# Two maximum tiles of a pair of steps as 64-row matmuls on the two halves of TensorE's rows, in a fused attention and feed-forward kernel

## The reference

```
q, k, v = (einsum('bsd,dhk->bshk', LN(x), W) + b  for q, k, v)
scores  = einsum('bqhk,bshk->bhqs', q, k) / sqrt(64)
attn    = softmax(scores)                       # over 2048 keys
ctx     = einsum('bhqs,bshk->bqhk', attn, v)
y       = LN(x) + einsum('bqhk,hkd->bqd', ctx, Wo) + bo
x       = x + LN(LN(y) * gamma + beta)
h       = silu(LN(x) @ wg.T) * (LN(x) @ wu.T)   # hidden width 768
out     = x + LN(h @ wd.T)
```

## Time and profile before

| | us |
|---|---|
| median of 3 runs | 2895.32 (2895.0 to 2895.43) |
| profiled execution, its own time | 2896.84 |
| its span | 2895.0 |
| opening, to about | 91 |
| 32 heads, about | 91 to 2472 |
| feed-forward part, about | 2472 to 2895 |

### The profile page before, as it was taken

The page is one execution under the profiler, slowest core; times in us unless marked ns, Lnnn a source line. Parts: engine busy times, 40 slices in busy tenths (PEclk is TensorE's granted clock), DMA queues, the critical chain, the costliest instruction groups (busy, mean ns, idle before and its releaser), DMA issues. The chain is left out here.

```text
span 2895.0 us, 82184 instructions
## 1 busy us (share of the span) xinstructions
PE 2762.3 (95%) x33632; PEld 1878.9 (65%) x33632; DVE 2318.1 (80%) x4121; ACT 2472.1 (85%) x4794; POOL 2295.1 (79%) x2023
## 2 busy tenths in 40 slices
PE   5899999999999999999999999999999999789997
PEld 4566666666666666666666666666666666567775
DVE  4688888988898888758888888888888887466664
ACT  4899999998999899889999999999999999555554
POOL 3789889988998888789889899999999999123434
PEclk9999999999999999999999999999999999799998
DMA  3322222111111111122222211111111211312110
GB/s 114 116 53 55 51 48 71 41 37 35 40 40 40 40 40 40 54 83 51 55 55 53 53 42 40 40 40 40 40 40 40 42 38 53 113 44 88 52 45 22
DMA packets 207945, 150.99 MB, mean 52 GB/s; under 512 B 158032, under 2 KB 181712, under 8 KB 206800
## 3 DMA queue, kind: packets, MB, share of 16 engines
q1 hardware_dynamic: 207568, 145.74, 20.3%
HBM read 55.26 MB, written 39.98 MB: 33 GB/s over the span
## 5 line engine op out<-in xcount | busy, mean ns | idle before, releaser
L524 POOL TENSOR_TENSOR p_l<-p_f,p_h 128x512 f16<-128x512 f32 x1536 | 1942.9, 1292 | 125.2 <-ACT p_h L592 120.6
L645 DVE TENSOR_REDUCE mx<-ps_aux 128x1 f32<-128x512 f32 x2048 | 1347.7, 681 | 331.5 <-PE ps_aux L793 330.7
L591 ACT ACTIVATE p_f<-ps_score 128x512 f32<-128x512 f32 x2048 | 1273.2, 624 | 32.1 <-PE ps_score L822 32.1
L592 ACT ACTIVATE p_h<-ps_score 128x512 f16<-128x512 f32 x2048 | 1282.1, 629 | 0.0
L847 PEld LDWEIGHTS ps_ctx<-v_hi_one_lo,p_h 128*128 128x128 f16 x16384 | 878.5, 97 | 253.1 <-issue 28.7
L847 PE MATMUL ps_ctx<-v_hi_one_lo,p_h 128*128 128x65 f16 (+1 forms) x16384 | 923.8, 194 | 2.1 <-issue 1.1
L847 PE MATMUL ps_ctx<-v_hi_one_lo,p_l 128*128 128x65 f16 x8192 | 792.0, 192 | 0.0
L821 PE MATMUL ps_score<-q_hilo,k_hihi 128*128 128x512 f16 x2048 | 779.5, 381 | 8.8 <-ACT v_new L553 5.2
L822 PE MATMUL ps_score<-q_hi_max,k_lo_one 65*128 65x512 f16 x2048 | 781.4, 382 | 0.0
L793 PE MATMUL ps_aux<-k_hihi,q_hilo 128*128 128x512 f16 x2048 | 621.3, 382 | 28.1 <-DVE mx L645 20.0
L663 DVE TENSOR_TENSOR p_l<-p_f,p_h 128x512 f16<-128x512 f32 x512 | 540.2, 1055 | 22.5 <-ACT p_h L592 22.5
(11 more groups left out here) (133 smaller groups left out, 2328.5 us busy)
## 6 DMA issues: line engine op xcount, KB each, us to landing
v_heads<-v_new SPq DMA_DIRECT2D x64, 258.0 KB, 2.1
v_hi_one_lo<-v_heads SPq DMA_DIRECT2D x32, 516.0 KB, 6.1
heads<-ctx_n SPq DMA_DIRECT2D x128, 128.0 KB, 2.0
x_all<-heads SPq DMA_DIRECT2D x8, 2048.0 KB, 7.9
k_hihi<-hi_st SPq DMA_DIRECT2D x62, 256.0 KB, 4.4
q_hi_max<-hi_st SPq DMA_DIRECT2D x32, 256.0 KB, 3.5
k_lo_one<-lo_st SPq DMA_DIRECT2D x32, 256.0 KB, 4.3
q_hilo<-hi_st SPq DMA_DIRECT2D x31, 256.0 KB, 3.2
```

What stands on the lines that cost most here:

```text
L524: nc.gpsimd.tensor_tensor(p_l[:, r], p_f[:, r], p_h[:, r], ALU.subtract).then_inc(lo_pool, 1)
L591: nc.scalar.activation(p_f[:, r], ps_score[:, bank], ACT.Exp, scale=exp_scale)
L592: nc.scalar.activation(p_h[:, r], ps_score[:, bank], ACT.Exp, scale=exp_scale).then_inc(exp_done, 1)
L645: nc.vector.reduce_max(mx[:, blk % 2, tt, ch:ch + 1], ps_aux[:, n % SIDE], AX_X).then_inc(max_read, 1)
```

## The change

Each maximum tile now multiplies high parts alone: 64 rows in place of 128. The first tile of a pair uses partitions 0 to 63 (q_hi in `qA`, k_hi in `kA`), the second partitions 64 to 127: k_hi stands there already, and a new tile `qC` (q_hi_below) holds a second copy of q_hi in its lower half. A fifth DMA in `fill_high` fills it. `max_tile` becomes `max_pair`: both bank waits stand ahead of the first of the two matmuls. The scores themselves are computed as before; the maximum that is subtracted leaves out the q_lo * k_hi part.

```
-HIGH_FILLS = 4
+HIGH_FILLS = 5
...
+        qC = [sb(f"q_hi_below{u}", [P, S], F16) for u in range(2)]
...
-                                 (kA[u][K:P, cols], hi_st[K:P, cols]), (qA[u][K:P, cols], lo_st[0:K, cols])):
+                                 (kA[u][K:P, cols], hi_st[K:P, cols]), (qA[u][K:P, cols], lo_st[0:K, cols]),
+                                 (qC[u][K:P, cols], hi_st[0:K, cols])):
                     sp.dma_start(dst, src).then_inc(full, 16)
...
-            def max_tile(g, blk, kt, n):
...
-                q = qA[u][:, blk * BLK:(blk + 1) * BLK].rearrange("k (p t) -> k t p", t=TB)[:, tt]
-                nc.tensor.matmul(ps_aux[:, n % SIDE], q, kA[u][:, ch * BLK:(ch + 1) * BLK],
-                                 start=True, stop=True).then_inc(aux_full, 1)
+            def max_pair(pair):
+
+                for g, blk, kt, n in pair:
+                    ch = kt // TB
+                    if g == 0:
+                        pe.wait_ge(high_first[max(ch, blk)], HIGH_FILLS * 16)
+                    elif blk == 0 and kt == 0:
+                        pe.wait_ge(high_full, high_filled(g))
+                    pe.wait_ge(*used.pop(0))
+                    used.append((max_read, g * STEPS + blk * KT + kt + 1 + SIDE))
+                for half, (g, blk, kt, n) in enumerate(pair):
+                    u = g % 2
+                    ch, tt = divmod(kt, TB)
+                    rows = slice(half * K, (half + 1) * K)
+                    q = (qA, qC)[half][u][rows, blk * BLK:(blk + 1) * BLK].rearrange("k (p t) -> k t p", t=TB)[:, tt]
+                    nc.tensor.matmul(ps_aux[:, n % SIDE], q, kA[u][rows, ch * BLK:(ch + 1) * BLK],
+                                     start=True, stop=True).then_inc(aux_full, 1)
...
-                    if kind == "max":
-                        max_tile(0, a, c, m)
+                    if kind == "max" and c % 2:
+                        max_pair([(0, a, c - 1, m - 1), (0, a, c, m)])
...
-                    for k in range(2) if t % 2 == 0 else ():
-                        for to, blk, of, n in maxima[t + k]:
-                            max_tile(to, blk, of, n)
+                    if t % 2 == 0 and maxima[t]:
+                        max_pair(maxima[t] + maxima[t + 1])
```

## The result

| | before | changed |
|---|---|---|
| median us | 2895.16 (4 runs, 2893.36 to 2895.43) | 2912.48 (4 runs, 2910.93 to 2913.37) |
| span of the profiled execution | 2895.0 | 2910.8 |
| ratio | | 1.0059, 95% interval 1.0047 to 1.0071 |

The change makes the kernel slower by 0.6%, 17 us. The forecast was 2776 us.

A forecast was written before the change was run, and what follows sets the result against it. TensorE was taken to bound regular heads; 4.0 us saved in each of 31.5 heads, less about 6 for norm work, gave 120 us, plus 1 for the opening: 2776 us against the median, range 2745 to 3020.

The forecast's parts named there:

- What bounds the kernel: In a regular head of 71.23 us TensorE is busy 71.22, so each 0.1 us it loses or saves shows.
- The maximum matmuls: In the heads, overlapping halves save one slot, 0.215 us a pair: 217 us less TensorE work over 1008 pairs.
- Going from 128 rows to 64 and back: Two row changes a pair, around the maximum tiles, at 30 ns each: 60 us of TensorE in all.
- The signs that I had named: Plain-pair gaps if switches are cheap: first maximum to score 0.22 to 0.30 us, last weighing to first maximum 0.03 to 0.06.
- The bounds, 0 and 163 ns: Limits for one row change on TensorE: nothing, or 163 ns if the array must be empty before the mode changes.
- Rival B: Each switch empties the array: a pair saves 215 ns and pays 325, giving 3007 us, far end 3235; chance 0.30.
- Rival D: Each switch partly drains the array, about 100 ns: 15 us gained, 2881 us; chance 0.10.
- rival C: The halves run in turn with no switching cost: tiles stay 0.43 us a pair, 2896 to 2906, say 2899; chance 0.12.
- What is late next: With TensorE at 66.3 us a regular head, engines' coupling adds 0.9: 67.2, a gain of 4.0 us.
- The waits: Both bank waits ahead of a pair's first matmul cost 0 with overlap, up to 10 us if tiles run in turn.
- The fifth fill: 31 more DMAs of 256 KB: nothing inside heads, a 1.2 us shift in the opening, counted as +1 us.
- High parts alone: The softmax shift differs a little, but exp() operations cost the same for any value: 0 us.

## Why the prediction was wrong, point by point

**What bounds the kernel.** Right: the distances between TensorE's starts at the maximum tiles and scores add up to 0.50 us more in a regular head, and the head is 0.50 longer; over 31.5 heads that is 16 of the 17 us.

**The maximum matmuls: saving of 0.215 us a pair by overlap.** Right. Both halves start together, and taking the overlap away cost 191 us.

**Going from 128 rows to 64 and back: 30 ns each.** This step failed, and it gave the wrong sign. It measured 95 to 105 ns in and 120 to 125 ns out, 0.22 us a pair in place of 0.06, so 222 us of TensorE in the heads in place of 60, against 217 saved. The signs that I had named tell it: first maximum to score 0.34 us (0.22 to 0.30 if a switch is cheap), last weighing matmul to first maximum 0.12 (0.03 to 0.06). The bounds, 0 and 163 ns, held; I chose the end by rows that did not switch to a part of the array (65 rows for 128, float32r for float16), and said so. Rival B put a cost at each switch and set the point from which it decides, 107 ns; the mean of the two is 110. Its price was too high, because it had the switch wait for the whole record (tails of 161 and 164 ns). Rival D, a partial drain of about 100 ns, was the nearest in the price, and its small gain came of 202 us paid in place of 222 and the longer first score tile (11 us). The total, 2912, lies in the wide range up to 3020 and nearest to rival C's 2899, but that is luck: the halves did not run in turn. What fills the bubble stays open. It may be a drain, or the weight load that is no longer hidden: its record, 0.11 and 0.10 us, is about as long as each bubble, and no run separates the two. I had left such a load small by the earlier trace rows, where load and matmul start together from idle; they do so after a change of rows too, so that row settles nothing.

The Trainium skill's page "TensorEngine Tiling (Array Packing)", section "Key Properties", says "Mode switching requires drain". A bubble at each change fits that; the far end that I had set for it, 163 ns, was too long. Part 3 of the Trainium skill's page "TensorE: Matmul & The Clock Gate" has matmuls on different row groups start about 4 ns apart, and the trace agrees: 3 ns by the median over the heads.

**What is late next: 67.2 us a head, a gain of 4.** This would have failed as well. With the switch taken away and half the matmuls gone the kernel was at 2879 us, not 2746 to 2760. I had summed busy time by engine (66, 63.5, 63 us) and set 0.9 us for their coupling. The first bound was the three banks of `ps_aux`: they are held from the matmul to the reduce, and a reduce comes late whenever VectorE has a burst. One bank a pair took 92 us off. I had seen the wait (25 us over all heads) and taken its smallness as a sign of room; with TensorE faster it grew. Even with banks enough the kernel was at 2787.5 us and a regular head at 69.4: VectorE was nearly full there, since the 63.5 us that I had taken as fixed became 67.8.

**The waits: 0.** The changed kernel probably loses 3 to 4 us by them. The bound I gave for tiles in turn, 10 us, fits the 7 us measured there.

**The fifth fill.** Right inside the heads; in the opening 0.7 us in place of 1.2, since the third chunk's fill began earlier.

**High parts alone: 0.** Nothing in the runs speaks against it; no run tests it by itself.

## What to carry to other kernels

Two 64-row matmuls side by side save one slot, and going to 64 rows and back costs about one slot of 512 columns: by these distances packing would pay from the second couple in a row, and it does not for one couple between full matmuls. When the engine that is the bound gets faster, ask which buffers it needs and when they come back: here three banks, two a pair, decided the next bound, and the sum of busy time did not show it. Nor is another engine's busy time fixed. A bank wait belongs directly ahead of the matmul that needs it: one matmul earlier, with 128-row tiles, it cost 7 us here.

## What the runs showed of the hardware that was not expected

The bubble of a change of rows was 0.095 to 0.105 us into 64 rows and 0.120 to 0.125 us out of them, at the 2.4 GHz level of the granted clock. It was the same after a 512-column matmul as after a 64-column one, and the same in sum with one 64-row tile, two side by side, or four. It is less than the 0.16 us by which a matmul's record outlasts the next start. Behind each change the weight load started with its matmul and not a slot ahead of it.
